# A two-layer decoder stack on one core: the constant warm-up products taken out of TensorE's program

## The reference

```
x = layernorm(x + linear_attention(x))                # 16 heads, causal by cumulative sums
x = layernorm(x + self_attention_and_cross_attention(x, context))   # softmax, two MLPs with GELU
x = layernorm(x + linear(fp6(x), fp6(weight)))        # both rounded to a 6-bit grid in blocks of 32
x = layernorm(x + recurrent_and_memory_block(x))      # conv gate, state scan, hashed memory, MLP
x = layernorm(x + cross_attention(x, context))        # 16 heads, softmax over the 1500 context tokens
x = layernorm(x + mixture_of_experts(x))              # 8 experts, top 2, and a shared one
```

## Time and profile before

| what | value |
|---|---|
| median of three runs | 749.22 us (748.0 to 750.85) |
| the profiled execution's own time | 749.95 us |
| its span, first to last instruction | 748.2 us |
| mean granted TensorE clock | 0.973 of full speed |
| PE busy | 666.2 us (89%) |
| DVE busy | 500.9 us (67%) |
| POOL busy | 340.5 us (46%) |
| ACT busy | 330.1 us (44%) |
| warm-up products, busy | 101.6 us (749) and 6.2 us (35) |

### The profile page before, as it was taken

The page is one execution under the profiler, slowest core; times in us unless marked ns, Lnnn a source line. Parts: engine busy times, 40 slices in busy tenths (PEclk is TensorE's granted clock), DMA queues, the critical chain, the costliest instruction groups (busy, mean ns, idle before and its releaser), DMA issues.

```text
span 748.2 us, 19799 instructions
## 1 busy us (share of the span) xinstructions
PE 666.2 (89%) x8821; PEld 464.6 (62%) x8821; DVE 500.9 (67%) x779; ACT 330.1 (44%) x449; POOL 340.5 (46%) x256
## 2 busy tenths in 40 slices
PE   9868888869999999999877777789999999999987
PEld 5535754547777777777644453466777777776752
DVE  3365832778888888886324464288889888888532
ACT  2123444243555466464242303425664664564441
POOL 1070435044876976764200144008667766845300
PEclk9998999998999999999999988999999999999998
DMA  9500003000000000000030000000000000000000
GB/s 255 199 0 1 4 1 125 1 1 2 2 3 2 2 3 2 2 3 2 2 136 4 1 0 1 0 2 1 3 2 2 3 2 2 3 2 2 2 1 12
DMA packets 3360, 14.81 MB, mean 20 GB/s; under 512 B 356, under 2 KB 484, under 8 KB 3276
## 3 DMA queue, kind: packets, MB, share of 16 engines
q1 hardware_dynamic: 3276, 13.56, 5.6%
HBM read 13.33 MB, written 0.23 MB: 18 GB/s over the span
## 4 chain that ended last, share of the span: by engine, by line
PE 67%; DVE 14%; ACT 9%; POOL 5%; issue 4%; DMA 1%; POOLq 0%; DVEq 0%; ACTq 0%
PE psum L840 16%; PE psum L749 8%; PE psum L798 5%; PE psum L198 5%; PE psum L791 5%; PE psum L793 4%; DVE scratch L918 3%; POOL scratch L903 2%; PE psum L213 2%; PE psum L206 2%; PE psum L740 1%; PE psum L731 1%; ACT scratch L865 1%; PE psum L755 1%; PE psum L599 1%
## 5 line engine op out<-in xcount | busy, mean ns | idle before, releaser
L903 POOL TENSOR_TENSOR scratch<-scratch 125x896 bf16<-125x896 f32 x136 | 232.3, 1718 | 150.4 <-ACT scratch L893 149.7
L893 ACT ACTIVATE scratch<-psum 125x896 f32<-125x896 f32 x192 | 173.9, 917 | 201.5 <-PE psum L840 199.7
L918 DVE TENSOR_REDUCE scratch<-psum 128x1 f32<-128x500 f32 x336 | 210.7, 672 | 17.6 <-PE psum L749 8.9
L840 PE MATMUL psum<-scratch 128*125 128x448 bf16 (+1 forms) x768 | 178.1, 357 | 4.0 <-issue 3.7
L749 PE MATMUL psum<-scratch 128*128 128x500 bf16 x336 | 127.1, 378 | 12.2 <-DVE scratch L918 7.3
L840 PEld LDWEIGHTS psum<-scratch 128*125 128x125 bf16 (+1 forms) x768 | 97.9, 137 | 34.8 <-issue 4.5
L791 PE MATMUL psum<-tok,scratch 125*128 125x65 bf16 x1344 | 109.4, 196 | 1.8 <-DVE kT L963 1.8
L793 PE MATMUL psum<-tok,scratch 125*128 125x64 bf16 x1344 | 108.8, 193 | 0.0
L791 PEld LDWEIGHTS psum<-tok,scratch 125*128 125x128 bf16 x1344 | 95.9, 97 | 14.0 <-issue 2.8
L198 PE MATMUL psum<-w_second 128*128 128x256 bf16 x749 | 101.6, 278 | 0.0
L793 PEld LDWEIGHTS psum<-tok,scratch 125*128 125x128 bf16 x1344 | 90.7, 99 | 14.6 <-issue 0.3
(11 more groups left out here) (307 smaller groups left out, 775.8 us busy)
## 6 DMA issues: line engine op xcount, KB each, us to landing
raw<-ctx_dram SPq DMA_DIRECT2D x4, 672.0 KB
w_third<-fifth_dram SPq DMA_DIRECT2D x3, 636.0 KB, 5.3
w_fourth<-fourth_dram SPq DMA_DIRECT2D x3, 566.5 KB, 6.6
w_third<-third_dram SPq DMA_DIRECT2D x2, 844.0 KB, 22.3
w_third<-third_dram SPq DMA_DIRECT2D x2, 843.5 KB, 20.4
w_first<-first_dram SPq DMA_DIRECT2D x1, 996.0 KB, 5.0
w_second<-second_dram SPq DMA_DIRECT2D x1, 834.0 KB, 6.8
w_third<-fifth_dram SPq DMA_DIRECT2D x1, 636.5 KB, 7.4
```

Of the source, the lines that this page charges most:

```text
L840: mm = nc.tensor.matmul(bank(S + f, HALF, CP), lhs[0:rows, CP * c:CP * c + CP], rhs[0:rows, HALF * f:HALF * f + HALF], start=(rows == 128) ...
L893: nc.scalar.activation(CR["p"][0:CP, n % RING, :].rearrange("p (f n) -> p f n", f=2), psum[0:CP, S:S + 2, 0:HALF], ACT.Exp).then_inc(self. ...
L903: ops.tensor_tensor(CR["pl"][0:CP, n % RING, :], CR["p"][0:CP, n % RING, :], p_high(n % RING), ALU.subtract).then_inc(done, 1)
L918: nc.vector.tensor_reduce(mxp[:, r, t:t + 1], bank(B, TB), X_AXIS, ALU.max).then_inc(self.aux_freed, 1)
```

## The change

Every call of `keep_warm` is removed, and the function and its counts with it. All waits, all real products and the programs of the other engines stay as they are. The diff, cut to its core:

```diff
-WARM, WARM2 = 6, 8
-WARM_A, WARM_B, WARM_C, WARM_D, WARM_F, WARM_G, WARM_H = 8, 8, 6, 6, 70, 16, 10
-        def keep_warm(n, b=2, constant=None):
-            constant = par("mean").bitcast(BF16) if constant is None else constant
-            for _ in range(n):
-                nc.tensor.matmul(bank(b, 256), constant[:, 0:128], constant, start=True, stop=True)
         def ln_pe(pe, k, x, ready, value):
...
-            if k:
-                keep_warm(WARM)
             ln_mean(pe, k)
         def ln_mean(pe, k):
...
-            if k != 13:
-                keep_warm(WARM2)
         def attn0_pe(pe):
             pe.wait_ge(warm_set, 1)
-            keep_warm(19, 0, warm_up)
...
-                        keep_warm(16 if p == 1 else 0, 7, warm_up)
...
-                        keep_warm(WARM_A, 7)
...
-                    keep_warm(WARM_B, 7)
...
-            keep_warm(20, 7)
...                                          # self_pe: scores, turned, outputs
-                    keep_warm((0, 16, 24, 6)[p], 7)
-                keep_warm((6, 30)[p == 3], 7)
-                keep_warm(WARM_D if p < PAIRS - 1 else 16, 7)
...                                          # Cross.pe_unit and Cross.run_pe
-                if kind == "M" and b == 0:
-                    keep_warm(3 if k else 12, 6)
-                    if n == 0:
-                        keep_warm(14)
-                    keep_warm(4, 2)
-                keep_warm(WARM_G, 2)
...                                          # fp6_pe_run
-            keep_warm(WARM_F, 5)
...                                          # mem_pe_run
-            keep_warm(20, 5)
-            keep_warm(15, 7)
-            keep_warm(12, 3)
-            keep_warm(12, 5)
-            keep_warm(8, 2)
...                                          # ahead of the output projection L1760
-            keep_warm(WARM_H, 2)
```

## The result

The changed kernel took 773.7 us (median of four runs, 771.53 to 774.8) against 749.41 for the kernel before, measured beside it: a ratio of 1.032, 95% interval 1.029 to 1.0351. It is 24 us slower. The forecast was 767.3, the range 748 to 790.

A forecast was written before the change was run, and what follows sets the result against it. TensorE's program was taken to set most of the time (67% of the chain of waits). 749.95 - 16.7 + 2.2 + 9.1 + 1.9 + 21.6 = 768.05, less 0.73 to the median: 767.3 us, range 748 to 790.

The forecast's parts named there:

- Rival A: Whole kernel: the clock holds through the norms, only about four more half-clock spells of 2.0 us; 743.5 us, chance 0.12.
- rival B: Whole kernel: a draw, half of the norms and blocks pay for half clock; 750.5 us, chance 0.10.
- C: Whole kernel cold: every norm and block pays, first attention's fetch stall at its upper bound; 794.8 us, chance 0.16.
- First attention, -8.9: First attention's pair loop: 13.4 us less without constant products, 4.5 charged for instruction stalls; net -8.9 us.
- Norms, +9.1: Layer norms: products at half clock, full price 1.7 us for numbers 1, 5 and 8, less for others; sum +9.1 us.
- Blocks, +21.6: Blocks of products entered at half clock or partly warm, and first chunks of both cross attentions, run longer: +21.6 us.
- Self-attention, -3.0: Self-attention: the chain's piece of 30 constant products goes, less 0.4 for small products at half clock: -3.0 us.
- single places, -4.1: Behind first cross attention's last unit, ahead of L1760, memory block, ahead of first chunk: constant products leave the chain, -4.1 us.
- fp6, +1.9: Fp6 layer: two sets of transposes and one product behind a bare DVE stretch run at half clock, +1.9 us.
- chunks, 0: The 96 chunks of each cross attention contain no constant product and keep the clock by themselves: no change.
- The start, +2.2: Kernel start: without the 19 products before the weights land, queries and keys begin at half clock, +2.2 us.
- The signs named beforehand: Signs: mean clock about 0.90, slices 5 to 8, most norm products near 1.8 us, first attention some 6 us earlier.

## Why the prediction was right, and where it was off

The direction and its cause were right, and the time was 6.4 us too low, which is 0.8% of it but a quarter of the change. Part of that nearness is luck: the first attention and the blocks were 6.1 and 6.5 us too cheap in the sum, and the norms 5.3 us too dear.

- *Half clock is the cost.* Shown, by the run with 32 rows, by the run with more products, and by L202 at 1.88 and L578 at 6.13 us. Rival A (few falls, 743.5) and rival B fall; C (all norms and blocks pay, 794.8) falls too.
- *First attention, -8.9.* Mis-sized: it measured -2.8. I charged 4.5 us for stalls and they were 6.15, and I reckoned the rest of the loop at full clock, while from 22.3 us on it ran at half. The fall at 22.35 us in the kernel before was in its trace, and the prediction leaves it out. The mechanism, instructions that arrive late while the loads run, was in the prediction and is shown by the runs with a hold and by the times of the instruction packets.
- *Norms, +9.1 (+8.4 with the 0.07 each).* Mis-sized: +3.1. I gave numbers 1, 5 and 8 both products at the full price; in 1 and 5 the first product still ran at 1.03, and the norms behind a block (0, 3, 4, 6, 7, 11, 12, 13) paid nothing at all, where I had given 3.4. I had read the idle in a norm as enough to lose the clock. In the changed kernel it fell mostly between norms and blocks, and the next block paid.
- *Blocks, +21.6.* Mis-sized: 28.1. Three projections behind an attention cost 7.2 us (L322 3.0, L590 the second time 1.8, L1760 2.4) and I had 0.3 for them. These had constant products right ahead of them, 20, 16 and 26, which I had booked only as time saved (in the loop's sum, -1.2 and -1.5) and not as something that may keep the block at full clock. The MLP's first block cost 2.9, 1.6 and 1.6 against 2.0 each, the experts 1.7 against 2.2, the first chunks 2.3 and 1.5 against 1.5 each.
- *Self-attention, -3.0, single places, -4.1, fp6, +1.9, chunks, 0.* Right within 0.4 us; the lag grows by nothing between the first 25 us of the chunks and their end. The start, +2.2, measured +1.4.
- *The signs named beforehand.* The mean clock (0.87 for about 0.90) and the slices came as said. Three signs did not: only 8 of the 26 norm products ran at 1.88 us, so their median is 1.03 and not 1.8; the first attention ended 1.5 us earlier and not 6; and the first cross attention's chunks grew by 2.3 us, over the 2 allowed. Of the blocks L599 and L603 only the first left 3.0 to 3.3 us; L603 took 3.02 all three times.
- *The skill's rule.* The Trainium skill (page "TensorE: Matmul & The Clock Gate", section "What's actually happening") says that the ramp penalty is under 1% of a typical kernel's span. It says so in a passage on the first matmuls of a kernel, and the trace agrees with that: the start cost 1.4 us, 0.2% of 748.2. The prediction took it as a bound on all that the clock costs, and as such it does not hold here: the lag above without its negative terms is 34 us, 4.6%.

What stays open: how much of the 25.0 us the three groups ahead of projections would bring back by themselves, since they were not put back alone. For the first of them two runs give a hint: without its 20 products the block took 1.8 us longer (the changed kernel with the loads held), and with 5 it took 3.43 us in the chain instead of 3.02, while the 20 take 2.29 us themselves. So this group may not pay for itself. Open too is why the kernel before with all of its loads held scatters over 10 us.

## What to carry to other kernels

A constant product on TensorE is worth its place where another engine's pass hides it and a block of real products follows; on the chain it costs 0.12 us each at full clock and must earn that in the block behind it. Before removing or adding such products, read them group by group: who waits when the group ends, and at which clock the next block runs. Here the clock's loss showed up mostly in the block behind the idle stretch (28.1 us), less in the small products next to it (3.1).

## What the runs showed of the hardware

- A product that reads 32 of 128 partitions took the same time as a full one (at most 416 ns against 422), but with it the clock was not held: PE busy 92%, clock 0.834, against 89% and 0.973.
- TensorE can run out of instructions. With loads at 364 GB/s it stood for 3.99 us among bursts of 64 small products, until 1.4 us after the next packet of instructions had landed; in the runs with loads held back a stall was 0.4 to 1.1 us. The stretch in the changed kernel:

```profile
19.90:23.80 3.90, 0.00 (x0) 0.00 (x0) 1.16 (x2) 0.00 (x0) 0.00 (x0) 0.80 0.94 364
```
